# The first two pairs of a graph layer share one transposed product T from the start

## The chip, the cores and the metric

One core of a Trainium2 chip. The metric is the device time of one execution in microseconds. TensorE (PE) does the products, ScalarE (ACT), VectorE (DVE) and GpSimd (POOL) work on tiles, SyncE (SP) issues the transfers.

## The reference, cut to what matters

```python
# x (32, 256, 512) f32, adj (32, 256, 256) int32, w, wq, wk (512, 512) f32
output = einsum('bni,io->bno', x, w)
q      = einsum('bni,io->bno', x, wq)
k      = einsum('bni,io->bno', x, wk)
alpha  = einsum('bno,bmo->bnm', q, k)
alpha  = maximum(alpha, 0) * (adj != 0)
alpha  = softmax(alpha, axis=1)
y      = x + einsum('bnm,bmo->bno', alpha, output)
out    = (y - mean(y)) / sqrt(var(y) + 1e-5)
```

## The kernel before

**The algebra.** The kernel never forms q and k. It forms G from wq and wk once (with a minus sign), then for each graph T = G times x transposed, the scores S from x and T, V = x w, and O = softmax times V. The last step adds x and normalises each row. Two graphs are one *pair*; 16 pairs are numbered 0 to 15. Two pairs, 2i in *slot* 0 and 2i+1 in *slot* 1, are one *group*.

**Three products for one.** Each operand is kept as two fp32r tiles, `hi` (a rounded copy, made by ACT) and `lo` (the remainder, whole minus `hi`, made by DVE or POOL). Each product of 128x128 by 128xN is three matmuls: hi·hi, lo·hi and hi·lo (`add_chunk`, L320 to L322).

**Seven products for eight.** T (from pair 1 on) and V (from pair 1 on) are computed with seven block products P1 to P7 in place of eight. These need sums of blocks of x (S1 to S4, tile `xs`, made by POOL in four steps where S2 needs S1 and S4 needs S2), sums of blocks of G (T1, T2, T3, D4, `sum_gt` on DVE) and of w (`w_sum` on POOL). Blocks of x are A11, A12, A21, A22, those of G B11, B12, B21, B22. P1 is A11 with B11, P2 A12 with B21, P4 A22 with D4, P5 S1 with T1, P6 S2 with T2, P7 S3 with T3, P3 S4 with B22. `t_half(Pn, c, pairs)` is one 128-row half of a product: two chunks, six matmuls. A T is 14 halves, 84 matmuls. P1, P6, P5 and P3 add up in the PSUM tile `chain`; ACT copies the running sum after P1, P6 and P5 (`parts`), and DVE adds P2 (`bank_z`), P7 and P4 (`bank_y`) to the copies (`sum_t`).

**In the steady state** the loop over groups 1 to 7 runs, on PE: T of both pairs (`fill_t`, 512 columns, both slots in one matmul), O of pair 2i-1, S of pair 2i, V of pair 2i, S of pair 2i+1, O of pair 2i, V of pair 2i+1.

**The start, which the change touches**, is outside that loop. On PE: seven warm-up matmuls (L650); rows 0 to 2 of V of pair 0, plain (L497 to L503); G (`fill_g`, four quarters j of four chunks each, in `g_bank[j]`); T of pair 0, plain with 512 columns (`fill_first_t`, 16 chunks, 48 matmuls); the last row of V of pair 0; S of pair 0; T of pair 1 alone with seven products and 256 columns (`fill_second_t`); O of pair 0; S of pair 1; V of pair 1; then group 1.

Every engine runs its instructions in the order written, and semaphores order the engines. The order of the start is written out by hand for ACT (L950 to L1020), DVE (L1271 to L1341) and POOL (L1473 to L1511). After G, ACT takes G's quarters out of PSUM (`split_g`, L925), DVE makes their remainders (L1235) and the sums (`sum_gt`, L1254 and L1260), ACT casts the sums (`split_gt`, L940) and DVE makes their remainders (L1025, `g_lo<-xn,g_hi`).

Semaphores named below: `g_lo_ready` and `gt_lo_ready` count finished remainders of G's blocks and of its sums, `x_summed[slot]` POOL's sums of x, `first_s_lo_ready` and `s_lo_ready` remainders of these, `t_lo_ready` finished blocks of T, `t_copied` and `t_summed` the copies and sums of T.

## Time and profile before

| | |
|---|---|
| time, median of 3 runs | 524.33 us (523.89 to 525.05) |
| the profiled execution: its own time | 523.82 us |
| its span, first to last instruction | 522.0 us |
| mean granted TensorE clock | 0.995 |
| busy: PE, PE weight load | 98%, 89% |
| busy: DVE, ACT, POOL | 71%, 62%, 49% |

The profiled execution's time is 1.8 us more than its span and 0.5 us less than the median. Matmuls are pipelined: a matmul's duration (0.39 us with 512 columns, 0.28 us with 256) is longer than the distance from one start to the next, which is what a stream of them costs. In a timeline a row gives the start, the duration, the engine, the line and the tiles; `x4` means that four instructions are merged and the duration is theirs together; a bracket gives the idle time ahead of it and who ended it.

### The profile page before, as it was taken

The page shows a single profiled execution, that of the slowest core. Times are in us where ns is not written, and L with a number is a line of the kernel's source. Part 1 is how long each engine was busy: PE and PEld are TensorE (multiplying, and loading weights), DVE is VectorE, ACT ScalarE, POOL GpSimd, SP SyncE. Part 2 cuts the span into 40 slices and gives each one's busy share as a digit, 9 for nine tenths or more (in the row PEclk, how much of TensorE's full clock was granted, in tenths as well). Part 3 has the DMA queues.
Part 4 walks back from the last instruction along what each step waited for, and adds up shares of the span by engine and source line. Part 5 has one row for each costly group of instructions (what it writes and reads, how often), then busy time and mean ns, then how long its engine had stood idle before and what let it go on. Part 6 is the DMA issues. An engine that isn't in the chain of part 4 may idle for free.

```text
span 522.0 us, 9934 instructions
## 1 busy us (share of the span) xinstructions
PE 511.8 (98%) x3259; PEld 466.2 (89%) x3259; DVE 368.1 (71%) x746; ACT 325.8 (62%) x747; POOL 258.1 (49%) x196
## 2 busy tenths in 40 slices
PE   8999999999999999999999999999999999999994
PEld 5889998899989998899988999889998999889994
DVE  4766846776948677586866778577684867757686
ACT  5566556476763857539574586638676385764583
POOL 0397875239635386155661486433962537710011
PEclk9999999999999999999999999999999999999998
DMA  7404241044430626025350333404351061502334
GB/s 261 182 0 161 90 155 62 21 125 152 154 115 20 213 69 241 20 52 189 109 206 21 127 138 118 166 20 161 120 200 61 20 221 60 201 1 69 133 130 192
DMA packets 30735, 62.05 MB, mean 119 GB/s; under 512 B 2048, under 2 KB 3072, under 8 KB 30720
## 3 DMA queue, kind: packets, MB, share of 16 engines
q1 hardware_dynamic: 30720, 61.87, 34.2%
q8 instruction: 7, 0.11, 0.1%
q14 instruction: 8, 0.07, 0.0%
HBM read 45.09 MB, written 16.78 MB: 119 GB/s over the span
## 4 chain that ended last, share of the span: by engine, by line
PE 94%; DVE 2%; ACT 1%; DMA 1%; issue 0%; POOLq 0%; POOL 0%; SPq 0%; DVEq 0%; ACTq 0%
PE o_bank L320 12%; PE o_bank L321 12%; PE o_bank L322 12%; PE chain L320 11%; PE chain L322 11%; PE chain L321 11%; PE bank_y L320 6%; PE bank_y L321 6%; PE bank_y L322 6%; PE bank_z L320 3%; PE bank_z L321 3%; PE bank_z L322 3%; DMA xn<-in_w 1%; PE chain L502 0%; PE chain L503 0%; ACT v_hi L755 0%
## 5 line engine op out<-in xcount | busy, mean ns | idle before, releaser
L1441 POOL TENSOR_TENSOR s_lo<-xs,s_hi 128x512 fp32r<-128x512 f32 x60 | 82.6, 1394 | 33.9 <-ACT s_hi L692 33.9
L1436 POOL TENSOR_TENSOR a_lo<-xt,a_hi 128x512 fp32r<-128x512 f32 x42 | 57.9, 1386 | 61.2 <-ACT a_hi L684 61.2
L322 PE MATMUL o_bank<-t_hi,a_lo 128*128 128x256 f32 x256 | 72.4, 283 | 0.0
L321 PE MATMUL o_bank<-t_lo,a_hi 128*128 128x256 f32 x256 | 72.4, 283 | 0.0
L320 PE MATMUL o_bank<-t_hi,a_hi 128*128 128x256 f32 x256 | 72.4, 283 | 0.0
L1432 POOL TENSOR_TENSOR xs<-xt 128x512 f32<-128x512 f32 x30 | 40.0, 1347 | 47.8 <-DMA xt<-in_x_t 30.1
L1446 POOL TENSOR_TENSOR rstd<-var_eps,minus_half 128x4 f32<-128x4 f32 x14 | 14.2, 1018 | 92.6 <-DVE var_eps L1122 92.6
L711 ACT COPY parts<-chain 128x256 f32<-128x256 f32 x90 | 33.2, 370 | 39.5 <-PE chain L322 38.4
L320 PE MATMUL chain<-w_hi,s_hi 128*128 128x256 f32 x180 | 51.0, 284 | 0.5 <-ACT parts L711 0.5
L322 PE MATMUL chain<-w_hi,s_lo 128*128 128x256 f32 x180 | 50.9, 283 | 0.0
L321 PE MATMUL chain<-w_lo,s_hi 128*128 128x256 f32 x180 | 50.9, 283 | 0.0
L321 PEld LDWEIGHTS o_bank<-t_lo,a_hi 128*128 128x128 f32 x256 | 49.1, 192 | 0.3
L320 PEld LDWEIGHTS o_bank<-t_hi,a_hi 128*128 128x128 f32 x256 | 49.1, 192 | 0.3
L322 PEld LDWEIGHTS o_bank<-t_hi,a_lo 128*128 128x128 f32 x256 | 49.1, 192 | 0.0
L320 PE MATMUL o_bank<-v_hi,p_hi 128*128 128x512 f32 (+1 forms) x126 | 48.5, 385 | 0.0
L321 PE MATMUL o_bank<-v_lo,p_hi 128*128 128x512 f32 (+1 forms) x126 | 48.5, 385 | 0.0
L1037 DVE TENSOR_TENSOR parts<-parts,bank_y 128x512 f32<-128x512 f32 (+1 forms) x32 | 20.7, 653 | 39.2 <-ACT parts L701 25.8
L322 PE MATMUL o_bank<-v_hi,p_lo 128*128 128x512 f32 (+1 forms) x126 | 48.4, 384 | 0.0
L1025 DVE TENSOR_TENSOR v_lo<-parts,v_hi 128x512 fp32r<-128x512 f32 x45 | 47.6, 1071 | 0.9 <-ACT v_hi L755 0.9
L1108 DVE SCALAR_TENSOR_TENSOR xn<-o_bank,xn 128x512 f32<-128x512 f32 x60 | 40.9, 683 | 8.4 <-PE o_bank L322 8.4
L701 ACT COPY parts<-chain 128x512 f32<-128x512 f32 x42 | 24.7, 588 | 34.6 <-PE chain L322 34.1
L783 ACT ACTIVATE c_b<-xn,neg_mean 128x512 f32<-128x512 f32 x58 | 41.9, 722 | 3.4 <-DVE neg_mean L1370 2.4
(222 smaller groups left out, 1628.9 us busy)
## 6 DMA issues: line engine op xcount, KB each, us to landing
xt<-in_x_t SPq DMA_DIRECT2D x64, 256.0 KB, 3.2
...
```

Of the source, the lines that this page charges most:

```text
L320: nc.tensor.matmul(dst, a[0], b[0], start=first, stop=False, skip_group_check=shared)
L321: nc.tensor.matmul(dst, a[0], b[1], start=False, stop=False, skip_group_check=shared)
L322: return nc.tensor.matmul(dst, a[1], b[0], start=False, stop=last, skip_group_check=shared)
L701: nc.scalar.copy(parts[:, PART[product], c], chain[:, c]).then_inc(t_copied, 1)
L711: nc.scalar.copy(parts[:, PART[product], c, 0], chain_v[:, c]).then_inc(v_copied, 1)
L783: nc.scalar.activation(squares, xn[:, slot, r], ACT.Square, bias=neg_mean[:, r:r + 1], accum_out=square_sum[:, r:r + 1]).then_inc(squared, 1)
L1025: return nc.vector.tensor_tensor(dst, whole, hi.bitcast(F32), ALU.subtract)
L1037: nc.vector.tensor_tensor(part, part, bank, ALU.add).then_inc(t_summed, 1)
L1108: nc.vector.scalar_tensor_tensor(out=xn[:, slot, r], in0=row.rearrange("q j n -> q (j n)"), scalar=1.0, in1=xn[:, slot, r], op0=ALU.mult, ...
L1432: nc.gpsimd.tensor_tensor(xs[:, s], a, b, op).then_inc(x_summed[slot], 1)
L1436: nc.gpsimd.tensor_tensor(a_lo[:, slot, u], xt[:, u], a_hi[:, slot, u].bitcast(F32), ALU.subtract).then_inc(a_lo_ready[slot], 1)
L1441: nc.gpsimd.tensor_tensor(s_lo[:, slot, s], xs[:, s], s_hi[:, slot, s].bitcast(F32), ALU.subtract).then_inc(s_lo_ready[slot], 1)
```

## The change

Pairs 0 and 1 become group 0 and get one T, with seven products and 512 columns, straight behind G.

- PE: `fill_first_t` is now 14 halves of both pairs, in the order P1 P1 P2 P7 P2 P7 P6 P6 P5 P5 P3 P3 P4 P4. S of pair 0 follows (`fill_first_s`), then the last row of V of pair 0, S of pair 1 (`fill_s_b(0)`), O of pair 0 (`fill_first_o`), V of pair 1.
- SP: the four blocks of pair 1 are loaded without a wait into space that is free at the start (`x1_raw`, in `soft` and `parts`), the adjacency of pair 0 behind them, and pair 2 as soon as pair 0's sums are made.
- Sums and remainders of x for both pairs are made in the start, by POOL and DVE, between the pieces of G. wk's parts move from `a_hi[:, 1]` to `s_hi[:, 1]`.
- B12 isn't split any more (only the plain T used it).

The diff, cut to its core:

```diff
+T_FIRST = {**T_DONE, (P1, 0): 1, (P1, 1): 2, (P2, 0): 3, (P7, 0): 4, (P2, 1): 5, (P7, 1): 6}
-FIRST_A, FIRST_S = (A11, A21, A12, A22), (S3, S2, S1, S4)
+FIRST_A, FIRST_S = (A11, A12, A22, A21), (S3, S1, S2, S4)
+FIRST_LO = {S3: 1, S2: 2}, {S1: 1, S4: 2}
+G_ORDER = (T3, T2, T1, D4)
+G_SUMMED = {(T1, 0): 1, (T1, 1): 2, (T3, 0): 3, (T2, 0): 4, (T3, 1): 5, (T2, 1): 6, (D4, 0): 7, (D4, 1): 8}
...
-        wk_hi, wk_lo = a_hi[:, 1], a_lo[:, 1]
+        wk_hi, wk_lo = s_hi[:, 1], s_lo[:, 1]
+        x1_raw = {A11: soft[:, 0:M], A21: soft[:, M:R], A12: parts[:, C22, 0], A22: parts[:, C22, 1]}
-        b12 = parts[:, 0, 0]
+        b12 = c12_b
...
 SP
+            for u in (A11, A21, A12, A22):
+                sp.dma_start(x1_raw[u], x_t[1].rearrange("q (u k n) -> q u k n", u=4, k=2)[:, u]).then_inc(
+                    x1_loaded[u], 16)
+            sp.dma_start(adj[:], adj_t[0].rearrange("q (r n) -> q r n", r=R)).then_inc(adj_loaded, 16)
             sp.wait_ge(a_lo_ready[0], 4)
-            for u in range(4):
-                load_block(1, u)
-            sp.dma_start(adj[:], adj_t[0].rearrange("q (r n) -> q r n", r=R)).then_inc(adj_loaded, 16)
+            for u in (A11, A21, A22, A12):
+                sp.wait_ge(x_summed[0], READ_BY[u])
+                load_block(2, u)
             sp.wait_ge(gt_lo_ready, 4)
             load_xn(0, 0)
...
 PE
-            def fill_second_t():
+            def fill_first_t():
+                both = slice(0, 2)
+                pe.wait_ge(g_lo_ready, 2)
+                pe.wait_ge(b_lo_ready, B_LO_FIRST[A11])
+                pe.wait_ge(v_lo_ready, 2)
+                t_half(P1, 0, both)
+                t_half(P1, 1, both)
+                pe.wait_ge(g_lo_ready, 4)
+                pe.wait_ge(b_lo_ready, B_LO_FIRST[A12])
+                t_half(P2, 0, both)
+                pe.wait_ge(gt_lo_ready, G_ORDER.index(T3) + 1)
                 xs_split(S3)
+                pe.wait_ge(v_lo_ready, 3)
+                t_half(P7, 0, both)
                 pe.wait_ge(t_summed, 1)
+                t_half(P2, 1, both)
+                pe.wait_ge(gt_summed, 8)
+                t_half(P7, 1, both)
...
+            def fill_first_s():
+                pe.wait_ge(t_lo_ready, T_LO[0][A12])
+                fill_scores(0, 0)
+                pe.wait_ge(t_lo_ready, 4)
+                fill_scores(0, 1)
...
             fill_g()
             fill_first_t()
+            fill_first_s()
             fill_last_of_first_v()
-            pe.wait_ge(t_lo_ready, 4)
-            fill_scores(0, 0)
-            fill_scores(0, 1)
-            fill_second_t()
-            fill_o_b(0, first=True)
-            pe.wait_ge(t_lo_ready, 4 + T_LO[0][A12])
-            pe.wait_ge(added, 2)
-            fill_scores(1, 0)
-            pe.wait_ge(t_lo_ready, 8)
-            pe.wait_ge(added, 3)
-            fill_scores(1, 1)
+            fill_s_b(0)
+            fill_first_o()
             fill_v(1, 1, first=True)
...
 ACT, behind split_first_v(0..2)
+            split_first_a(A11)
+            split_first_s(0, S3)
+            split_first_a(A12)
+            split_g(0)
+            split_g(1)
+            split_first_s(0, S1)
+            split_first_s(0, S2)
+            split_first_a(A22)
+            split_first_a(A21)
+            split_g(2)
+            split_first_s(0, S4)
+            split_g(3)
+            split_gt(T3)
+            split_first_s(1, S3)
+            split_gt(T2)
+            split_first_s(1, S1)
+            copy_first_t(P1, 0)
+            copy_first_t(P1, 1)
+            split_first_s(1, S2)
+            split_gt(T1)
+            split_gt(D4)
+            split_first_s(1, S4)
... then the copies of P6 and P5, split_t_a, copy_c12, split_wt(T1, T3, T2), split_t_b and exponent(0, r),
... split_first_v(3), split_p(0, r), split_wt(D4), split_a(1, 0, u), split_s(1, 0, s)
 DVE, behind split_first_v(0..2)
+            split_first_b(A11)
+            split_first_s(0, S3)
+            split_first_b(A12)
+            split_g(0)
+            sum_gt(T1, 0)
+            split_g(1)
+            sum_gt(T1, 1)
+            split_first_s(0, S2)
+            split_g(2)
+            sum_gt(T3, 0)
+            sum_gt(T2, 0)
+            split_g(3)
+            sum_gt(T3, 1)
+            sum_gt(T2, 1)
+            split_first_s(1, S3)
+            split_gt(T3)
+            sum_gt(D4, 0)
+            sum_gt(D4, 1)
+            sum_t(0, A11, 0, first=True)
+            split_gt(T2)
+            split_first_s(1, S2)
+            split_gt(T1)
... then sum_t(A11, 1), split_gt(D4), sum_t(A22, 0 and 1), split_t_a(A11), split_t_a(A22),
... sum_t(A21, 0), sum_t(A21, 1), split_t_a(A12), split_t_a(A21), mask(0, 0), relu_max, split_t_b(A11), mask(0, 1),
... split_t_b(A12), relu_max, split_t_b(A22), split_t_b(A21), split_first_v(3), invert(0), split_p(0, r)
 POOL, behind the same wait on qk_lo_ready
+            sum_first_x(0, S3)
+            sum_first_x(0, S1)
+            sum_first_x(0, S2)
+            sum_first_x(1, S3)
+            split_first_s(0, S1)
+            sum_first_x(1, S1)
+            sum_first_x(0, S4)
+            sum_first_x(1, S2)
+            split_first_s(0, S4)
+            sum_first_x(1, S4)
+            split_first_s(1, S1)
+            split_first_s(1, S4)
+            split_first_a(A22)
+            split_first_a(A21)
... then w_sum as before, sum_x(1, 0, s), the remainders of w's sums (D4 last), split_a(1, 0, u), split_s(1, 0, s)
```

The new helpers are single instructions with their waits:

```python
# ACT
def split_first_s(slot, s):
    act.wait_ge(x_summed[slot], S_SUMMED[s])      # S_SUMMED = {S3: 1, S1: 2, S2: 3, S4: 4}
    if slot == 1:
        act.wait_ge(g_filled, K)
    nc.scalar.copy(s_hi[:, slot, s], xs[:, s]).then_inc(s_hi_ready[slot], 1)
# DVE
def split_first_s(slot, s):
    dve.wait_ge(s_hi_ready[slot], FIRST_S.index(s) + 1)
    rest(s_lo[:, slot, s], xs[:, s], s_hi[:, slot, s]).then_inc(first_s_lo_ready[slot], 1)
def split_first_b(u):
    dve.wait_ge(a_hi_ready[1], FIRST_A.index(u) + 1)
    rest(a_lo[:, 1, u], x1_raw[u], a_hi[:, 1, u]).then_inc(b_lo_ready, 1)
```

`sum_first_x(1, s)` on POOL also waits until the slot 0 remainder of the same s is done, because both slots use one tile `xs[:, s]`.

## Rows read from the trace of the kernel before

**Rows 1.** The page: busy time by engine, and the chain that ended last.

```profile
PE 511.8 (98%) x3259; PEld 466.2 (89%) x3259; DVE 368.1 (71%) x746; ACT 325.8 (62%) x747; POOL 258.1 (49%) x196
...
PE 94%; DVE 2%; ACT 1%; DMA 1%; issue 0%; POOLq 0%; POOL 0%; SPq 0%; DVEq 0%; ACTq 0%
```

**Rows 2.** The timeline of PE, 0 to 82 us: first matmuls of its stages.

```profile
1.45 3.36 PE L650 MATMUL o_bank<-s_hi 128*128 128x512 f32 x7 [1.45 <-DVE s_hi L1271]
...
25.55 0.39 PE L320 MATMUL chain<-a_hi,g_hi 128*128 128x512 f32 x1
...
36.43 0.39 PE L320 MATMUL o_bank<-w_hi,a_hi 128*128 128x512 f32 x1
...
39.15 0.28 PE L320 MATMUL o_bank<-t_hi,a_hi 128*128 128x256 f32 x1
...
44.90 0.28 PE L320 MATMUL bank_y<-s_hi,g_hi 128*128 128x256 f32 x1
...
60.92 0.28 PE L320 MATMUL o_bank<-t_hi,a_hi 128*128 128x256 f32 x1
...
66.67 0.28 PE L320 MATMUL chain<-w_hi,a_hi 128*128 128x256 f32 x1
...
77.54 0.40 PE L320 MATMUL bank_y<-s_hi,g_hi 128*128 128x512 f32 x1
```

**Rows 3.** The timeline of POOL, 0 to 82 us.

```profile
18.55 2.54 POOL L1432 TENSOR_TENSOR xs<-xt 128x512 f32<-128x512 f32 x2 [17.72 <-DVE a_lo L1025]
21.17 1.29 POOL L1432 TENSOR_TENSOR xs<-xs,xt 128x512 f32<-128x512 f32 x1
22.61 1.29 POOL L1432 TENSOR_TENSOR xs<-xt,xs 128x512 f32<-128x512 f32 x1
26.93 5.07 POOL L1481 TENSOR_TENSOR a_lo<-xt,a_hi 128x512 fp32r<-128x512 f32 x4 [3.03 <-ACT a_hi L970]
31.96 5.95 POOL L1441 TENSOR_TENSOR s_lo<-xs,s_hi 128x512 fp32r<-128x512 f32 x4
...
59.37 5.51 POOL L1436 TENSOR_TENSOR a_lo<-xt,a_hi 128x512 fp32r<-128x512 f32 x4
64.84 5.04 POOL L1441 TENSOR_TENSOR s_lo<-xs,s_hi 128x512 fp32r<-128x512 f32 x4
69.83 2.56 POOL L1432 TENSOR_TENSOR xs<-xt 128x512 f32<-128x512 f32 x2
74.91 1.30 POOL L1441 TENSOR_TENSOR s_lo<-xs,s_hi 128x512 fp32r<-128x512 f32 x1 [2.52 <-ACT s_hi L692]
```

**Rows 4.** The timeline of DVE, 0 to 82 us.

```profile
18.34 1.28 DVE L1025 TENSOR_TENSOR v_lo<-chain,v_hi 128x512 fp32r<-128x512 f32 x2
...
27.65 0.41 DVE L1260 SCALAR_TENSOR_TENSOR xn<-o_bank,parts 128x256 f32<-128x256 f32 x1
...
31.05 3.20 DVE L1025 TENSOR_TENSOR g_lo<-xn,g_hi 128x512 fp32r<-128x512 f32 x2 [2.00 <-ACT g_hi L940]
```

**Rows 5.** The timeline of ACT, 0 to 82 us.

```profile
17.95 0.60 ACT L923 CAST v_hi<-bank_y 128x512 fp32r<-128x512 f32 x1
...
25.75 0.60 ACT L936 ACTIVATE g_hi<-bank_z 128x512 fp32r<-128x512 f32 x1 [2.12 <-PE bank_z L322]
...
30.40 2.19 ACT L940 CAST g_hi<-xn 128x512 fp32r<-128x512 f32 x4
```

**Rows 6.** The timeline of DVE, 150 to 162 us, behind the T of a group in the loop.

```profile
158.45 0.69 DVE L1037 TENSOR_TENSOR parts<-parts,bank_y 128x512 f32<-128x512 f32 x1 [0.59 <-PE bank_y L322]
159.05 0.68 DVE L1025 TENSOR_TENSOR t_lo<-chain,t_hi 128x512 fp32r<-128x512 f32 x1
```

**Rows 7.** Windows at the end of the kernel: start:end, length, busy us of PE, PEld, DVE, ACT, POOL (instructions), granted clock, DMA share, GB/s.

```profile
514.00:516.00 2.00, 0.94 (x8) 0.73 (x7) 1.90 (x9) 1.91 (x5) 0.00 (x0) 1.00 0.00 0
516.00:518.00 2.00, 0.00 (x0) 0.00 (x0) 1.67 (x6) 0.84 (x2) 1.39 (x2) 0.81 0.00 0
518.00:522.00 4.00, 0.00 (x0) 0.00 (x0) 0.71 (x2) 0.00 (x0) 0.00 (x0) 0.50 0.68 262
```

More of the change, by code:

```diff
@@ L711, in copy_v, with split_t_a @@
                 nc.scalar.copy(parts[:, PART[product], c, 0], chain_v[:, c]).then_inc(v_copied, 1)
-            def split_t_a(i, u):
-                if u == A11:
+            def split_t_a(i, u, first=False):
+                if u == A11 and not first:
                     act.wait_ge(s_filled, 4 * i)
@@ L733, in split_t_b @@
                 if u == A12:
[L734 removed]
+                    act.wait_ge(c12_copied, i + 1)
                 whole = c12_b[:] if u == A12 else parts[:, BLOCK_AT[u], :, 1]
[L736 to L744 removed]
                 nc.scalar.copy(t_hi[:, u], whole).then_inc(t_hi_ready, 1)
@@ new lines, in _ @@
+            copy_first_t(P6, 0)
+            copy_first_t(P6, 1)
+            split_t_a(0, A11, first=True)
+            copy_first_t(P5, 0)
+            copy_first_t(P5, 1)
+            split_t_a(0, A22)
+            split_t_a(0, A12)
+            copy_c12(0, first=True)
+            split_t_a(0, A21)
+            for b in W_ORDER[:-1]:
+                split_wt(b)
+            split_t_b(0, A11)
+            split_t_b(0, A12)
+            exponent(0, 0)
+            exponent(0, 1)
+            split_t_b(0, A21)
@@ L979, in _ @@
+            exponent(0, 2)
+            exponent(0, 3)
+            split_t_b(0, A22)
             split_first_v(R - 1)
[L980 to L981 removed]
             for r in range(R):
[L983 to L994 removed]
@@ L995, in _ @@
-            split_second_t(A11)
-            split_second_t(A22)
-            split_second_t(A12)
-            split_second_t(A21)
+                split_p(0, r, first=True)
+            split_wt(D4)
             for u in (A21, A11, A12, A22):
@@ new lines, in _ @@
+            sum_gt(T2, 1)
[6 more added lines that the diff above has]
+            split_first_s(1, S2)
+            split_gt(T1)
+            sum_t(0, A11, 1, first=True)
+            split_gt(D4)
+            sum_t(0, A22, 0, first=True)
+            sum_t(0, A22, 1, first=True)
+            split_t_a(0, A11)
+            split_t_a(0, A22)
+            sum_t(0, A21, 0, first=True)
@@ new lines, in _ @@
+            sum_t(0, A21, 1, first=True)
+            split_t_a(0, A12)
+            split_t_a(0, A21)
+            dve.wait_ge(x_summed[1], 4)
+            dve.wait_ge(a_lo_ready[1], 2)
+            mask(0, 0, first=True)
+            relu_max(0, 0)
+            relu_max(0, 1)
+            split_t_b(0, A11)
+            mask(0, 1, first=True)
+            split_t_b(0, A12)
+            relu_max(0, 2)
+            relu_max(0, 3)
+            split_t_b(0, A22)
+            split_t_b(0, A21)
+            split_first_v(R - 1)
@@ L1312, in _ @@
             invert(0)
-            one = slice(1, 2)
-            sum_t(0, A11, 0, one)
             split_p(0, 0)
-            sum_t(0, A11, 1, one)
-            for r in range(1, R):
-                split_p(0, r)
-            sum_t(0, A22, 0, one)
-            sum_t(0, A22, 1, one)
-            split_second_t(A11)
-            split_second_t(A22)
-            sum_t(0, A21, 0, one)
-            sum_t(0, A21, 1, one)
-            split_second_t(A12)
-            residual(0, 0, 0, 0)
-            residual(0, 0, 0, 1)
```

299 lines of the change are left out of this document (126 added, 173 removed).

## The prediction

> **What bounds the kernel now.** I read the page's busy times and its chain first. PE is busy 98% of the span and makes up 94% of the chain that ended last, and no other engine is above 71% [rows 1]. So time is PE's instructions plus the places where PE has nothing to do, and the change touches only the stretch behind G. I then read PE's timeline as a row of stages [rows 2]: T of pair 0 starts at 25.55, V's last row at 36.43, S of pair 0 at 39.15, T of pair 1 at 44.90, S of pair 1 at 60.92, V of pair 1 at 66.67, and group 1 at 77.54. That is 51.99 us from the end of G to group 1.
>
> Two prices come out of it. With 512 columns 48 matmuls take 36.43 - 25.55 = 10.88 us, 0.227 each. With 256 columns 48 take 44.90 - 39.15 = 5.75 us, 0.120 each [rows 2]. Priced so, the work of the stretch is 10.88 (T of pair 0) + 2.72 (V's row, 12 matmuls) + 5.75 (S) + 84 x 0.120 = 10.08 (T of pair 1) + 24 x 0.227 = 5.44 (O) + 5.75 (S) + 10.08 (V) = 50.70. What is left, 51.99 - 50.70 = 1.29 us, is PE's idle time there. The stretch is nearly full, because each chain of other engines has PE work of another pair ahead of it.
>
> **What the change removes.** T of both pairs becomes 84 matmuls of 512 columns, 19.04 us, for 10.88 + 10.08 = 20.96. That is 1.92 us less. With no idle time at all, a further 1.29 would go, 3.21 in all. Everything else PE does (S, O, V, the loop) keeps its count and shape. A loss can only be new idle time of PE, and above 3.21 us of it the change costs time.
>
> **What the change adds: five places.** I follow the written order of each engine with these prices. A POOL operation on 512 elements costs 1.27 (5.07 for four), an ACT cast 0.60 to 0.62, 0.52 from start to start when they follow each other (2.19 for four), a DVE remainder with its whole in PSUM 0.64 (1.28 for two), a half-width sum on DVE 0.41 [rows 3 to 5]. A DVE remainder with both inputs in SBUF beside a busy POOL is dearer: two took 3.20, and the four POOL operations that ran then took 5.95 in place of 5.07, so POOL loses 0.44 to each [rows 3, 4].
>
> *Place 1, ahead of P2.* P1's two halves run from 25.55 to 28.27 (12 x 0.227). P2 needs all four quarters of G as remainders, and ACT's cast of the last quarter now stands behind its cast of S4 of pair 0. G's last quarter was in PSUM and its cast began at 25.75 [rows 5]. But S4 is POOL's seventh operation, POOL starts at 18.55 as before [rows 3], and 7 x 1.27 brings it to 27.4 at the earliest. DVE's four remainders from SBUF in that stretch (A11 and A12 of pair 1, S3 and S2 of pair 0) take 4 x 0.44 = 1.8 from POOL. The sum of S3 for pair 1 overwrites the tile that the second of them reads and waits some 0.3 for it. S4 is then ready at 29.5, its cast at 30.1, G's last cast at 30.75, and the DVE remainder at 31.45. PE idles from 28.27 to 31.45, **3.2 us**. Without any contention it is 27.4 + 0.6 + 0.6 + 0.65 = 29.25, 1.0 us. If DVE's remainders also push each other (1.6 each from the row, so that the one of S2 comes a POOL operation late) it is up to 4.0.
>
> The Trainium skill (SBUF — State Buffer, Who interferes with whom) says that a DVE instruction with two SBUF inputs and a GpSimd instruction that reads SBUF exclude each other for the whole instruction. Taken by that, POOL would lose a full DVE instruction each time and place 1 would be about 1 us longer; in this trace POOL lost 0.44 each and not the 0.69 of such an instruction. I keep the row.
>
> *Place 2, ahead of P7.* Behind that remainder stand T3's second half-sum (0.41), ACT's cast (0.62), ACT's cast of S3 for pair 1 (0.52 more), DVE's remainder of that and then of T3 (0.60 and 0.69 without contention), and some 0.3 of steps between engines: 3.0 to 3.2 us. P2's half covers 1.36. PE idles **1.7 us**; 1.5 with no contention, 2.9 if both DVE remainders meet POOL at 1.6 each. From here each product is ready in time: T2, T1 and D4 come 0.6 to 3 us apart and PE needs one every 2.72.
>
> *Place 3, between T and S.* S needs A12 of T, whose remainder DVE makes behind the last sum, and that sum waits for PE's last half. In the loop the same two rows follow the last half of T: the sum starts at 158.45 and the remainder ends at 159.73 [rows 6], 1.3 us plus the step from PE. There O of another pair covers it. Here nothing does: **1.4 us**, firmly (1.3 to 1.5).
>
> *Place 4, in S of pair 1.* Behind S of pair 0 PE has only V's last row, 2.72 us, for DVE and ACT to mask, take maxima, and split T of pair 1 again. By the written order DVE waits with A22 for ACT's cast, which stands behind two exponents. I get A21 done 0.3 us after PE wants it: **0.3 us** (0 to 1.5, the upper one if POOL is still at w's remainders).
>
> *Place 5, ahead of group 1.* POOL's remainder of w's D4 stands ahead of pair 2's eight remainders, and ACT casts D4 only behind the softmax of pair 0, at about 65.6. POOL starts the eight at 66.9; it started them at 59.37 before [rows 3]. They and two sums ran to 72.39, and the remainder of S3 for pair 3 ended at 76.21 after 2.52 of idle time that the delay uses up [rows 3]. Now I get 66.9 + 13.1 + 1.3 = 81.3, against PE's arrival at about 81. With contention by two DVE remainders of the next pair: **0.6 us** (0 to 1.5). The DMAs moved ahead (four blocks of pair 1 and the adjacency) stand in SP's queue behind wk as before, and only lose a wait; pair 2's blocks start at about 29 and not 44.6. I cost them at nothing: all are wanted 10 us after they land.
>
> **Sum.** -1.92 - 1.29 + 3.2 + 1.7 + 1.4 + 0.3 + 0.6 = +4.0 us. Against the profiled execution's 523.82 that is 527.8. The median of the runs stands 0.5 higher, so 524.33 + 4.0 = **528.3 us**. The ends of the terms give +0.6 to +8.1.
>
> **The rivals.**
> *The sums come in time (faster).* The one mechanism is that ACT does not wait for S4, so that place 1 is nil and place 2 at most 0.7; the point of decision is idle time below 3.21 - 1.05 = 2.16 us. Then it is 522.5. Against it: POOL's seven operations at 1.27 alone pass P1's end, and place 3 alone takes 1.4. Chance 0.05.
> *Light contention.* POOL and DVE miss each other, places 1, 2 and 3 take 1.0, 1.5 and 1.3, the others little: +0.6 to +1.7, 525.5. For it: POOL's 5.07 row has no contention. Against it: DVE has SBUF remainders back to back while POOL never stops. Chance 0.15.
> *As summed,* 528.3, chance 0.50.
> *The clock falls in place 1,* by the rows and by the page's rule above, 529.6. Against it: P1 before and P2 behind keep PE partly at work. Chance 0.22.
> *POOL's lateness goes on into group 1,* and PE waits again for S2's and S4's remainders there: 530.5 to 533. Against it: POOL is busy half the span [rows 1]. Chance 0.08.
>
> **Range and chances.** The likeliest case alone runs from 526.8 to 529.8. For eight in ten I go from 525.4, inside light contention, to 531.0. About 0.2% (1.05 us) is what a measurement of this kernel can tell from no change. Light contention lies half within it: same 0.09. Faster has 0.05, slower 0.86.
>
> **What the profile after would show.** G ends at 25.55 and P1 at 28.3. PE's first half of P2 starts at about 31.5, released by DVE's remainder of G's last quarter, behind an ACT cast that POOL's seventh `xs` released. P7 starts at 34.5, S at 50.9, V of pair 1 at 71, group 1 at 81.5, and from there the loop's period is the same. I am wrong if ACT casts G's last quarter near 26, if POOL's sums end before 27, or if group 1 starts before 78.

## The result, and the profile after

The changed kernel takes 531.49 us (median of 5 runs, 531.25 to 533.7), the kernel before 525.05 (5 runs, 523.89 to 525.4). The ratio is 1.0145, interval 1.0131 to 1.016 (it is taken over the runs and isn't the quotient of the two medians, which is 1.012). By the medians the change is 6.4 us slower, where +4.0 was predicted, and 0.5 us above the end of the range. The profiled execution is the longest of the five: 533.70 us, span 531.9. It is 9.88 above that of before.

The page of the kernel after, for [rows 1]:

```profile
PE 513.9 (97%) x3211; PEld 465.5 (88%) x3211; DVE 380.8 (72%) x750; ACT 330.0 (62%) x750; POOL 258.3 (49%) x198
...
PE 89%; DVE 2%; issue 1%; ACT 1%; POOL 1%; POOLq 0%; DVEq 0%; ACTq 0%
```

PE fell from 94% of the chain to 89%. So the loss is idle time of PE. The view of the waits, engine PE, from 25 to 90 us, names it; each row gives who waited, for whom, the sum, the number of times and the longest. Kernel after:

```profile
PE bank_y L329 <- DVE parts L1066: 3.1, 1, 3.1
PE bank_y L329 <- DVE g_lo L1047: 2.8, 1, 2.8
PE bank_z L329 <- DVE g_lo L1252: 1.5, 1, 1.5
PE o_bank L329 <- DVE t_lo L1047: 1.5, 1, 1.5
```

The same view of the kernel before, 25 to 78 us, has one row:

```profile
PE chain L320 <- ACT parts L711: 0.5, 1, 0.5
```

The first is at place 5, which the prediction priced at 0.6; the others are places 2, 1 and 3. The timeline of PE in the kernel after, for [rows 2], shows where they lie:

```profile
27.00 0.39 PE L329 MATMUL chain<-a_hi,g_hi 128*128 128x512 f32 x1
...
31.33 0.50 PE L329 MATMUL bank_z<-a_hi,g_hi 128*128 128x512 f32 x1 [1.46 <-DVE g_lo L1252]
...
35.77 0.50 PE L329 MATMUL bank_y<-s_hi,g_hi 128*128 128x512 f32 x1 [2.76 <-DVE g_lo L1047]
...
52.48 0.38 PE L329 MATMUL o_bank<-t_hi,a_hi 128*128 128x256 f32 x1 [1.45 <-DVE t_lo L1047]
...
84.28 0.39 PE L329 MATMUL bank_y<-w_hi,a_hi 128*128 128x256 f32 x1 [3.10 <-DVE parts L1066]
...
85.97 0.63 PE L329 MATMUL bank_y<-s_hi,g_hi 128*128 128x512 f32 x1
86.40 0.63 PE L330 MATMUL bank_y<-s_lo,g_hi 128*128 128x512 f32 x1
...
106.49 0.39 PE L329 MATMUL o_bank<-v_hi,p_hi 128*128 128x512 f32 x1
```

Two things beside the waits are to be seen. G ended at 27.00 and not at 25.55, because the matmuls behind the warm-up ran at half speed until 10.3 us (starts 0.43 apart in place of 0.23). And group 1 began at 85.97 with starts 0.43 apart again: T of group 1 took 106.49 - 85.97 = 20.52 where it took 19.06 before. From O of group 1 on the pieces are those of before: O starts 9.88 us later than in the kernel before (96.61), and the whole execution is 9.88 us longer.

Place 1 by engine, kernel after, for [rows 3] to [rows 5]; POOL, then ACT, then DVE:

```profile
18.65 2.55 POOL L1476 TENSOR_TENSOR xs<-xt 128x512 f32<-128x512 f32 x2 [17.81 <-DVE s_lo L1047]
...
28.12 1.28 POOL L1476 TENSOR_TENSOR xs<-xt,xs 128x512 f32<-128x512 f32 x1
```

```profile
29.44 0.62 ACT L956 CAST s_hi<-xs 128x512 fp32r<-128x512 f32 x1 [4.34 <-POOL xs L1476]
29.96 0.59 ACT L937 ACTIVATE g_hi<-bank_y 128x512 fp32r<-128x512 f32 x1
```

```profile
30.59 0.69 DVE L1252 SCALAR_TENSOR_TENSOR g_lo<-bank_y,g_hi 128x512 fp32r<-128x512 f32 x1 [2.32 <-ACT g_hi L937]
...
32.82 1.19 DVE L1047 TENSOR_TENSOR s_lo<-xs,s_hi 128x512 fp32r<-128x512 f32 x1 [0.88 <-ACT s_hi L956]
33.93 1.78 DVE L1047 TENSOR_TENSOR g_lo<-xn,g_hi 128x512 fp32r<-128x512 f32 x1
```

This is the chain of place 1 as written down: POOL's seventh sum ends at 29.40, ACT's cast of S4 and then of G's last quarter follow, DVE's remainder ends at 31.28 (31.45 in the prediction). The last two rows are place 2: both remainders met POOL, at 1.19 and 1.78 in place of 0.60 and 0.69.

And the wait of 3.1 us, DVE and then POOL of the kernel after:

```profile
79.27 4.36 DVE L1047 TENSOR_TENSOR a_lo<-xt,a_hi 128x512 fp32r<-128x512 f32 x1 [4.89 <-ACT a_hi L690]
83.55 0.68 DVE L1066 TENSOR_TENSOR parts<-parts,bank_y 128x512 f32<-128x512 f32 x1
```

```profile
67.83 5.26 POOL L1504 TENSOR_TENSOR a_lo<-xt,a_hi 128x512 fp32r<-128x512 f32 x4
73.03 5.08 POOL L1509 TENSOR_TENSOR s_lo<-xs,s_hi 128x512 fp32r<-128x512 f32 x4
78.05 2.58 POOL L1500 TENSOR_TENSOR xs<-xt 128x512 f32<-128x512 f32 x2
80.56 1.30 POOL L1509 TENSOR_TENSOR s_lo<-xs,s_hi 128x512 fp32r<-128x512 f32 x1
81.79 1.29 POOL L1500 TENSOR_TENSOR xs<-xs,xt 128x512 f32<-128x512 f32 x1
83.25 1.51 POOL L1500 TENSOR_TENSOR xs<-xt,xs 128x512 f32<-128x512 f32 x1 [0.17 <-POOL xs L1500]
```

DVE's remainder of A11 of pair 3 (both inputs in SBUF) lasted 4.36 us. POOL worked without a break under it, at its undisturbed 1.29 each, and the remainder ended 0.5 us after POOL's first pause (83.08). I call this the *hold*. The sum that P4 of V of pair 1 needs stands behind it on DVE. In the kernel before the same remainder fell into a pause of POOL (its row of 2.52 us idle ahead of 74.91 in [rows 3]); kernel before, DVE:

```profile
74.34 0.69 DVE L1025 TENSOR_TENSOR a_lo<-xt,a_hi 128x512 fp32r<-128x512 f32 x1 [5.91 <-ACT a_hi L684]
```

The windows view of the kernel after, 80 to 90 us, has a fall of the clock like the one of [rows 7]: after PE's wait for P4 the granted clock is 0.83 in the mean, between its levels of 2.4 and 1.2 GHz.

```profile
80.00:90.00 10.00, 6.90 (x34) 5.84 (x34) 9.89 (x11) 4.84 (x10) 6.39 (x5) 0.83 0.24 89
```

Behind T in the loop the rows of [rows 6] are the same in the kernel after (168.33 0.69, then 168.93 0.68).

### The profile page after: what moved, and what is told of

It reads as the page before. It is cut to its first block, busy times and chain, and to the rows that moved or that the text cites. A ratio compares the mean times of both kernels' runs of the same rounds, so it can differ in the third digit from the quotient of the medians.

```text
span 531.9 us, 9835 instructions
## 1 busy us (share of the span) xinstructions
PE 513.9 (97%) x3211; PEld 465.5 (88%) x3211; DVE 380.8 (72%) x750; ACT 330.0 (62%) x750; POOL 258.3 (49%) x198
## 4 chain that ended last, share of the span: by engine, by line
PE 89%; DVE 2%; issue 1%; ACT 1%; POOL 1%; POOLq 0%; DVEq 0%; ACTq 0%
PE o_bank L329 11%; PE o_bank L330 11%; PE o_bank L331 11%; PE chain L329 11%; PE chain L331 10%; PE chain L330 10%; PE bank_y L329 6%; PE bank_y L330 5%; PE bank_y L331 5%; PE bank_z L331 3%; PE bank_z L329 3%; PE bank_z L330 3%; POOL xs L1476 1%; DVE parts L1066 0%; DVE g_lo L1047 0%
## 5 line engine op out<-in xcount | busy, mean ns | idle before, releaser
L1509 POOL TENSOR_TENSOR s_lo<-xs,s_hi 128x512 fp32r<-128x512 f32 x56 | 75.9, 1372 | 40.0 <-ACT s_hi L698 40.0
L1059 DVE TENSOR_TENSOR parts<-parts,bank_y 128x512 f32<-128x512 f32 x32 | 22.0, 688 | 43.5 <-ACT parts L707 25.8
L1500 POOL TENSOR_TENSOR xs<-xt 128x512 f32<-128x512 f32 x28 | 36.9, 1329 | 25.2 <-DMA xt<-in_x_t 25.2
L1145 DVE TENSOR_SCALAR xn<-xn,neg_mean,rstd 128x512 f32<-128x512 f32 x56 | 41.6, 764 | 10.1 <-POOL rstd L1514 10.1
L1047 DVE TENSOR_TENSOR v_lo<-parts,v_hi 128x512 fp32r<-128x512 f32 x45 | 46.0, 1032 | 1.0 <-ACT v_hi L759 1.0
L749 ACT CAST t_hi<-parts 128x512 fp32r<-128x512 f32 x24 | 14.9, 622 | 51.2 <-PE o_bank L331 51.2
```

What stands on the lines that cost most here:

```text
L749: nc.scalar.copy(t_hi[:, u], whole).then_inc(t_hi_ready, 1)
L1047: return nc.vector.tensor_tensor(dst, whole, hi.bitcast(F32), ALU.subtract)
L1059: nc.vector.tensor_tensor(part, part, bank, ALU.add).then_inc(t_summed, 1)
L1145: nc.vector.tensor_scalar(xn[:, slot, r], xn[:, slot, r], neg_mean[:, r:r + 1], rstd[:, r:r + 1], ALU.add, ALU.mult).then_inc(normed, 1)
L1500: nc.gpsimd.tensor_tensor(xs[:, s], a, b, op).then_inc(x_summed[slot], 1)
L1509: nc.gpsimd.tensor_tensor(s_lo[:, slot, s], xs[:, s], s_hi[:, slot, s].bitcast(F32), ALU.subtract).then_inc(s_lo_ready[slot], 1)
```

## The experiments

In the table "over before" is the difference of the medians on the same chip; the ratio is again taken over the runs. Where I compare with the changed kernel, its three comparisons gave +6.4, +10.4 and +7.9 over before, so a gain against one of them alone says little below 4 us. The diffs below are against the changed kernel unless said otherwise.

| kernel | median us (range, runs) | before | over before | ratio, interval |
|---|---|---|---|---|
| after_again | 534.47 (534.08 to 534.95, 4) | 524.04 | +10.4 | 1.0188, 1.0171 to 1.0206 |
| e1_sum_first | 530.23 (530.17 to 530.29, 4) | 524.04 | +6.2 | 1.011, 1.0093 to 1.0127 |
| e2_d4_early | 529.41 (528.85 to 530.39, 4) | 524.04 | +5.4 | 1.0091, 1.0072 to 1.011 |
| e3_g_before_s4 | 531.08 (529.97 to 532.13, 4) | 524.04 | +7.0 | 1.0127, 1.0102 to 1.0152 |
| e4_fillers | 531.75 (531.13 to 532.1, 4) | 524.31 | +7.4 | 1.0131, 1.011 to 1.0152 |
| e5_port_gap | 530.99 (529.59 to 531.17, 4) | 524.31 | +6.7 | 1.0118, 1.0099 to 1.0137 |
| e6_act_order | 526.44 (526.29 to 529.56, 8) | 524.31 | +2.1 | 1.0045, 1.0026 to 1.0064 |
| e7_three | 525.15 (524.79 to 526.88, 10) | 524.31 | +0.8 | 1.0017, 1.0006 to 1.0029 |
| e8_v_between | 527.68 (524.7 to 527.92, 7) | 524.32 | +3.4 | 1.0051, 1.0032 to 1.0069 |
| e9_row_pieces | 525.59 (524.77 to 526.98, 10) | 524.32 | +1.3 | 1.0027, 1.0015 to 1.0038 |
| after_third | 532.48 (531.35 to 533.06, 4) | 524.63 | +7.9 | 1.0145, 1.0127 to 1.0163 |
| e5_again | 531.32 (528.35 to 532.37, 6) | 524.63 | +6.7 | 1.0121, 1.0099 to 1.0144 |
| e10_tail_order | 523.72 (523.33 to 525.62, 12) | 524.06 | -0.3 | 0.999, 0.9978 to 1.0003 |
| e11_v_first | 522.57 (522.28 to 522.77, 7) | 523.90 | -1.3 | 0.9973, 0.9961 to 0.9984 |

### The changed kernel once more

> The changed kernel once more, to see which of its stalls come in every execution. Theory A (a port that DVE did not get): DVE's remainder of A11 for pair 3, ahead of group 1, again takes about 4.4 us and the first matmul of P4 in V of pair 1 waits about 3 us; time 531.0 to 531.8. Rival (that one execution was unlucky): the remainder takes under 2 us, P4 waits under 1 us, and that execution's time is near 528.5.

It took 534.47, 3.0 us more than in the first comparison and more than either theory gave. Its profile (own time 534.95) has the same four waits and the hold again, at 4.25. The warm-up ended on time here and place 1 had its full length, and the clock fell twice. Waits of PE and DVE's row, then the windows, kernel after_again:

```profile
31.20 0.50 PE L329 MATMUL bank_z<-a_hi,g_hi 128*128 128x512 f32 x1 [2.68 <-DVE g_lo L1252]
35.63 0.79 PE L329 MATMUL bank_y<-s_hi,g_hi 128*128 128x512 f32 x1 [2.35 <-DVE g_lo L1047]
...
85.57 0.39 PE L329 MATMUL bank_y<-w_hi,a_hi 128*128 128x256 f32 x1 [2.99 <-DVE parts L1066]
```

```profile
80.67 4.25 DVE L1047 TENSOR_TENSOR a_lo<-xt,a_hi 128x512 fp32r<-128x512 f32 x1 [5.02 <-ACT a_hi L690]
```

```profile
30.00:40.00 10.00, 6.44 (x18) 4.70 (x19) 8.40 (x11) 5.75 (x11) 6.97 (x6) 0.66 0.08 26
...
80.00:90.00 10.00, 7.01 (x41) 6.22 (x40) 9.25 (x10) 5.94 (x12) 7.35 (x6) 0.84 0.39 143
```

P2 starts at the same absolute time in both (31.33, 31.20), though T started at 27.00 in one and 25.64 in the other. So in these two a late warm-up costs little: place 1 hides it.

### Place 5: the sum ahead of the remainder, D4's cast early, a pause on POOL

```diff
 e1, DVE                       e2, ACT
-            split_b(1, A11)   +            split_wt(D4)
             sum_v(1, A22)                  for r in range(R):
+            split_b(1, A11)                    split_p(0, r, first=True)
             sum_v(1, A11)     -            split_wt(D4)
```

> Only DVE's order ahead of group 1 differs: the sum that P4 of V waits for stands ahead of the remainder of A11 and no longer behind it. Theory A: the wait of P4 (3.1 us) goes, PE's clock no longer falls behind it (1.5 us), and the time drops by 3 to 4.6 us, to 527 to 528.5. Rival (group 1 waits for POOL's remainders anyway, as the prediction had it in place 5): PE waits at group 1's first halves instead, and the drop is under 2 us.

> ACT casts w's D4 ahead of the four softmax casts of pair 0 and not behind them, so that POOL starts pair 2's remainders earlier by 1.7 to 3.2 us. Theory B (POOL's lateness is what hurts ahead of group 1): its stream is over before DVE comes with the remainder of A11, the remainder is short, and the drop is 3 to 4.6 us. Rival (it only moves the softmax casts back by one cast): O of pair 0 starts 0.5 us later and nothing is gained at P4, 0 to +0.5 us.

Both take P4's wait away, as both theories said, and against after_again on the same chip they save 4.2 and 5.1 us (3 to 4.6 expected of each). Against the +6.4 and +7.9 of the other two comparisons of the changed kernel they save 0.2 and 1.7 (e1), 1.0 and 2.5 (e2). In e1 the remainder takes 1.68, but behind the sum. In e2 POOL starts earlier, has a pause when the remainder comes, and it takes 0.69 again. Kernel e2_d4_early, DVE, then POOL:

```profile
80.92 0.69 DVE L1047 TENSOR_TENSOR a_lo<-xt,a_hi 128x512 fp32r<-128x512 f32 x1 [5.00 <-ACT a_hi L690]
```

```profile
78.35 2.56 POOL L1500 TENSOR_TENSOR xs<-xt 128x512 f32<-128x512 f32 x2
81.48 1.30 POOL L1509 TENSOR_TENSOR s_lo<-xs,s_hi 128x512 fp32r<-128x512 f32 x1 [0.57 <-ACT s_hi L698]
```

Group 1 starts at 84.01 and 84.11 with no wait ahead of P4, 3.2 us earlier than in after_again, and its T runs at the full clock from the start (starts 0.23 apart), which is 1.4 more.

```diff
 e5, POOL
             sum_x(1, 1, S1)
+            pool.wait_ge(b_lo_ready, 3)
             split_s(1, 1, S3)
```

> POOL waits, ahead of its remainder of S3 for pair 3, until DVE's remainder of A11 for the same pair is done. Theory A (DVE is kept from the port by POOL's unbroken row of operations): the remainder takes at most 1.8 us in place of 4.3, P4's wait in V of pair 1 falls from 3 us to under 0.8, and the time drops by 2 to 4 us. Rival (the 4.3 us have another cause, such as data that is late): the remainder still takes over 3 us and the time rises by what POOL now loses.

With POOL held back for that one remainder it takes 1.89 (from 79.23), PE's wait shrinks from 3.10 to 0.63, and group 1 starts at 83.31. But e3 and e4 below, whose DVE and POOL have the order of the changed kernel, have no hold either (1.78 and 1.89), and e5's median is within 0.8 us of e4's. The rows fit theory A: in both holds and in e5 the remainder ended 0.55 us after POOL's first pause began (at 83.08, 84.37 and 80.58). But an execution of the edit without a hold shows nothing by itself where the unedited order also runs without one, and the time didn't show the expected gain of 2 to 4 us either: +6.7 lies above the +6.4 of the first comparison. So that POOL's row keeps DVE out is argued from the rows; how often it does is the next question.

### Is the hold in every execution?

The changed kernel and e5 on one chip, and two more single executions of the changed kernel, each with its profile:

> The changed kernel, unedited, beside e5's edit on one chip. In two profiles DVE's remainder of A11 of pair 3 was held from 79.27 and 80.67 for 4.36 and 4.25 us; in e3 and e4, whose DVE and POOL orders are the same, it took 1.78 and 1.89. Theory A (the hold is a property of this order and timing, and is in nearly every execution of the changed kernel): the profile shows it again at over 4 us, group 1 starts 3.4 us after V's end of work, and the median lies 2.5 to 4.5 us above that of e5_again. Rival B (it is a chance event that profiled executions happened to show): the profile may show 1.8 us, and the median lies within 1.5 us of e5_again.

> POOL waits for the remainder before its own third operation, as in e5_port_gap. The hold can't occur. By both theories the remainder takes under 2 us and the time is 5 to 7 us above the kernel before; theory A puts it 2.5 to 4.5 us below after_third, rival B within 1.5 us.

> The changed kernel, one more profile on the same chip. Theory A: the remainder takes over 4 us. Rival B: under 2 us here or in after_third or after_fifth. Where it takes under 2 us the time should be about 2.6 us less by the wait and 1.4 by the clock.

> The changed kernel, one more profile on the same chip, for the same question. Theory A: over 4 us. Rival B: a mixture over the three.

Theory A fell. The median of after_third is 1.2 us above that of e5_again, the intervals of their ratios overlap, and the remainder took 1.78, 1.80 and 1.89 in the three profiles (own times 532.90, 531.50, 530.77). The hold is in two of five profiles of the changed kernel. The orders are the same; in after_fifth DVE gets through at the first border between two POOL operations, behind the two sums, and POOL's next operation grows to 1.73. Without a hold PE's wait is short, and it is again for DVE's sum behind that remainder. Kernel after_fifth, PE, then DVE, then POOL:

```profile
82.57 0.39 PE L329 MATMUL bank_y<-w_hi,a_hi 128*128 128x256 f32 x1 [0.62 <-DVE parts L1066]
```

```profile
80.03 1.89 DVE L1047 TENSOR_TENSOR a_lo<-xt,a_hi 128x512 fp32r<-128x512 f32 x1 [4.90 <-ACT a_hi L690]
```

```profile
78.82 2.55 POOL L1500 TENSOR_TENSOR xs<-xt 128x512 f32<-128x512 f32 x2
81.32 1.73 POOL L1509 TENSOR_TENSOR s_lo<-xs,s_hi 128x512 fp32r<-128x512 f32 x1
83.01 1.30 POOL L1500 TENSOR_TENSOR xs<-xs,xt 128x512 f32<-128x512 f32 x1
```

The clock varies as much: it stayed at 1.00 in after_fifth in every window, through waits of 1.92 and 2.77 us, and was lowest in after_third. Windows, kernel after_third:

```profile
30.00:40.00 10.00, 6.71 (x15) 4.85 (x16) 8.21 (x11) 6.21 (x12) 6.95 (x6) 0.59 0.07 26
40.00:50.00 10.00, 10.00 (x41) 8.15 (x41) 2.90 (x5) 2.87 (x5) 9.84 (x8) 0.90 0.28 105
```

### Place 1: who waits on ACT

```diff
 e3, ACT
             split_g(2)
-            split_first_s(0, S4)
             split_g(3)
+            split_first_s(0, S4)
             split_gt(T3)
```

> ACT casts G's last quarter ahead of S4 of pair 0. Theory C (place 1 of the prediction: PE waits at P2 because ACT waits for POOL's seventh sum): PE's wait ahead of P2 (1.6 us in the profile after, 1.5 more hidden by a late warm-up) goes, P7 starts 1.5 to 2.2 us earlier, because the cast of T3 still stands behind S4, and the time drops by 1.5 to 2.2 us. Rival (T3's own chain sets P7): P7 starts less than 0.5 us earlier and the time stays within 0.5 us.

Kernel e3_g_before_s4, PE:

```profile
28.99 0.43 PE L329 MATMUL bank_z<-a_hi,g_hi 128*128 128x512 f32 x1
...
34.34 0.79 PE L329 MATMUL bank_y<-s_hi,g_hi 128*128 128x512 f32 x1 [3.78 <-DVE g_lo L1047]
```

Place 1 is gone (P2 starts at 28.99 with no wait), so its cause was S4 on ACT. But P7 comes only 1.3 us earlier than in after_again (34.34 for 35.63), a little less than theory C had: T3's cast still stands behind S4's, and PE's wait went there, 3.78 us long. The clock fell in it (0.66 from 30 to 40 us), and S of pair 0 starts only 0.3 earlier (53.61 for 53.94), though T had started 0.6 later here (26.27 for 25.64). The time is 3.4 below after_again, more than the 1.5 to 2.2 expected, but nearly all of that is place 5, where there was no hold here (1.78), P4 waits 0.52, and T of group 1 runs at the full clock.

```diff
 e6, ACT
-            split_first_s(0, S4)
             split_g(3)
-            split_gt(T3)
             split_first_s(1, S3)
+            split_gt(T3)
             split_gt(T2)
+            split_first_s(0, S4)
             split_first_s(1, S1)
```

> ACT's order between G and T alone: G's last quarter, S3 of pair 1, T3 and T2 are all cast ahead of S4 of pair 0. Theory C (that one cast, behind POOL's seventh sum, makes places 1 and 2): P7's first matmul starts at 31 to 32.5 and not at 35.7, PE's clock doesn't fall there, and the time drops by 4 to 6 us against the changed kernel. Rival (DVE's port collisions or POOL's sums set T3 anyway): P7 starts later than 34 and the drop is under 2 us.

S4 goes behind T3 and T2 as well. Waits of PE, kernel e6_act_order:

```profile
28.79 0.50 PE L329 MATMUL bank_z<-a_hi,g_hi 128*128 128x512 f32 x1 [0.32 <-DVE g_lo L1252]
31.74 0.50 PE L329 MATMUL bank_y<-s_hi,g_hi 128*128 128x512 f32 x1 [1.29 <-DVE g_lo L1047]
48.44 0.39 PE L329 MATMUL o_bank<-t_hi,a_hi 128*128 128x256 f32 x1 [1.45 <-DVE t_lo L1047]
78.03 0.38 PE L329 MATMUL bank_y<-w_hi,a_hi 128*128 128x256 f32 x1 [0.62 <-DVE parts L1066]
```

P7 starts at 31.74, as theory C said. The two places shrink from 5.9 us together (in after_again, by the starts, as in the table further down) to 2.1, the clock stays at 1.00 in every window of the profile, and the time is 2.1 us above before, 4.3 us less than the smallest excess of the changed kernel.

> The order of e6_act_order, the sum of e1_sum_first ahead of the remainder, and w's D4 cast as in e2_d4_early. If the places add up, the gains do too: 4 to 6 us, 3 us and up to 1 us off, which gives 523 to 526, about the kernel before. Rival (what is won at the front is given back, because POOL is then as late as before ahead of group 1): the gain is no more than e6_act_order's.

e7 is e6 with e1 and e2. P4's wait goes, and +0.8 us is left, inside the expected 523 to 526 us. Its waits are 0.37 (P2), 1.30 (P7) and 1.45 (S), 3.1 together, as much as the change can save.

### Is it the clock, or the idle time?

```diff
 e4, PE: idle products of 512 columns, which nothing reads
             t_half(P1, 1, both)
+            pe.wait_ge(gt_summed, 2)
+            fillers(10)
             pe.wait_ge(g_lo_ready, 4)
...
             t_half(P2, 0, both)
+            fillers(10)
...
+                    pe.wait_ge(added, R)
+                    fillers(11, w_hi[:, 0])       # ahead of P4 of V of pair 1
```

> The changed kernel with extra matmuls whose results nobody reads, at the places where PE waits: 10 of 512 columns ahead of P2, 10 ahead of P7, 11 ahead of P4 in V of pair 1 (about 2.3 us each, less than each wait). Theory D (PE's clock falls because of these waits, and that costs 1.5 to 3 us): the granted clock stays at its upper level from the warm-up to the end, and the time is 1.5 to 4 us below the changed kernel's of the same day (531.5 to 534.5), though no wait is any shorter. Rival (the clock falls for another reason, or costs nothing since the waits hide it): same time within 0.5 us, or more by the fillers.

The granted clock is 1.00 in each window from 10 to 90 us (the page's mean 0.997), and the kernel is still 7.4 us slower than before. So the waits cost most of what the change loses without any fall of the clock; 2.5 us of the 7.4 are the idle products ahead of P4, where the wait without a hold is 0.8. The saving of 1.5 to 4 us that I expected isn't shown: the changed kernel did not run on this chip, and +7.4 lies between its +6.4 and +10.4. What a fall of the clock costs is read from rows instead, in the table of the section on the prediction.

### Cover for the three places

```diff
 e9, PE, against e7: the row's four chunks as cover
             t_half(P1, 1, both)
+            pe.wait_ge(gt_summed, 1)
+            last_row_chunk(0)
...
             t_half(P2, 0, both)
+            last_row_chunk(1)
+            last_row_chunk(2)
...
             t_half(P7, 0, both)
...
             fill_first_t()
+            last_row_chunk(3)
             fill_first_s()
-            fill_last_of_first_v()
             fill_s_b(0)
 e8, PE, against e9: V of pair 1 between the two S
             fill_first_s()
+            fill_v(1, 1, first=True)
             fill_s_b(0)
             fill_first_o()
-            fill_v(1, 1, first=True)
```

In e8 the written orders of ACT, DVE and POOL follow PE's new order, with D4 cast ahead of T's second half.

> e7_three with only the chunks of V's last row moved into the three waits, and nothing in their old place between S of pair 0 and S of pair 1. Theory E: the waits at P2, P7 and ahead of S shrink by some 2.7 us together, and the same 2.7 us come back as a wait in S of pair 1, whose T still has to be split: time within 1 us of e7_three. Rival (the row was no cover, S of pair 1 is ready anyway): 2 to 2.7 us less than e7_three, 522.5 to 523.

> Built on e6_act_order and e1_sum_first, with PE's work laid where it waits: the four chunks of V's last row go one ahead of P2, two ahead of P7 and one ahead of S of pair 0, and V of pair 1 goes between S of pair 0 and S of pair 1, as the loop has it; ACT, DVE and POOL follow that order. Theory E (what the change lacked was PE work as cover, the 1.9 us of work that it saves are real): PE's idle time behind G falls to under 1.5 us, group 1 starts at 75 to 76.5 and the time is 1 to 2.5 us below the kernel before, 521.8 to 523.3. Rival (POOL can't have pair 2's and 3's remainders ready that early): group 1 waits for them and starts at 77.5 or later, no gain.

In e9 places 1 and 2 are covered, place 3 shrinks to 0.77, and a wait of 1.76 comes up ahead of S of pair 1, which the row had covered; the clock fell behind it (0.83 from 50 to 60 us). Kernel e9_row_pieces, PE:

```profile
48.30 0.39 PE L329 MATMUL o_bank<-t_hi,a_hi 128*128 128x256 f32 x1 [0.77 <-DVE t_lo L1050]
56.08 0.39 PE L329 MATMUL o_bank<-t_hi,a_hi 128*128 128x256 f32 x1 [1.76 <-DVE t_lo L1050]
```

It stands 1.3 above before and e7 0.8, so the two are within 1 us of each other, as theory E had it. In e8 V of pair 1 covers that chain too, but the tail's order, made for the old place of V, leaves a wait of 2.12 at group 1's P1, and the clock falls there (0.83 from 80 to 90). Group 1 started at 76.89, and the expected time below the kernel before was missed by far: +3.4. The seven executions of e8 are one of 524.70 with a mean granted clock of 0.997 and six of 527.12 to 527.92 with 0.993 or 0.994.

```diff
 e10, ACT, against e8
-            for r in range(R):
-                exponent(1, r)
+            act.wait_ge(s_filled, 4)
             split_a(1, 1, A11)
-            split_s(1, 1, S3)
             split_a(1, 1, A12)
+            exponent(1, 0)
+            split_s(1, 1, S3)
+            for r in range(1, R):
+                exponent(1, r)
 e10, DVE
             residual(0, 0, 0, 0)
             split_b(1, A11)
-            for r in range(1, R):
-                residual(0, 0, 0, r)
+            residual(0, 0, 0, 1)
             split_b(1, A12)
-            means(0, first=True)
+            residual(0, 0, 0, 2)
             invert(1)
+            residual(0, 0, 0, 3)
             split_v(1, A12, V_AT[1])
+            means(0, first=True)
 e11, DVE, against e10
             split_b(1, A12)
+            split_v(1, A12, V_AT[1])
+            invert(1)
             residual(0, 0, 0, 2)
-            invert(1)
             residual(0, 0, 0, 3)
-            split_v(1, A12, V_AT[1])
             means(0, first=True)
```

> e8_v_between with two orders mended ahead of group 1: ACT casts A11, A12 and S3 of pair 3 ahead of three of the four exponents of pair 1, and DVE makes the last residual row and the remainder of V's A12 ahead of the means. In e8_v_between PE waited 0.6 us ahead of group 1, 2.3 us ahead of its P1 and its clock fell there. Theory E: both waits go, the clock holds, and the time is 521.5 to 523, under the kernel before. Rival (the start only hands its lateness on to the next place, whatever the order): another wait of 1 us or more appears in group 1 and the time stays at 524 or above.

Group 1 starts at 75.57, 1.97 us earlier than in the kernel before. One wait of 1.41 at its P1 gives most of it back, and the time equals that of before within the interval: not the 521.5 to 523 of theory E, and the new wait is the one that the rival had. The remainder that it waits for starts on DVE at 77.60, behind two rows of the residual. Kernel e10_tail_order, PE:

```profile
78.51 0.49 PE L329 MATMUL chain<-a_hi,g_hi 128*128 128x512 f32 x1 [1.41 <-DVE v_lo L1052]
```

> DVE's remainder of A12 of V of pair 1 moves ahead of the third and fourth rows of the residual of pair 0; nothing else differs from e10. In e10 PE stood 1.57 us at group 1's first product (76.93 to 78.51), which wants the bank that this remainder reads; ACT's cast for it had ended at 76.36, and DVE made the remainder only at 77.60, behind two rows and the inversion. Theory A (what is left after place 1 to 5 is the order of DVE's work, not its amount): the remainder starts at about 76.4 and the first product at about 77.1 to 77.3, so the wait shrinks from 1.57 to about 0.3 us, the profiled span falls by 1.2 to 1.3 us and the time to about 522.5, 1.5 below the kernel before (ratio 0.997). Rival B (the 1.2 us only moves: the third and fourth rows of the residual free banks or columns later and PE waits in group 1 for them): the time stays at e10's, within 0.3 us of the kernel before.

Theory A held in the main. The remainder starts at 76.72, the wait is 0.22, the span is 0.8 us shorter than e10's (1.2 to 1.3 expected), and the median is 522.57, 1.3 us below the kernel before; the whole interval lies below 1. Kernel e11_v_first, PE:

```profile
48.74 0.39 PE L329 MATMUL o_bank<-t_hi,a_hi 128*128 128x256 f32 x1 [0.77 <-DVE t_lo L1052]
77.64 0.49 PE L329 MATMUL chain<-a_hi,g_hi 128*128 128x512 f32 x1 [0.22 <-DVE v_lo L1052]
```

From T to group 1 e11 has about as much idle time as the kernel before (1.4 and 1.3 us) and takes 1.8 us less. So the change's 1.92 us of saved work are real, and what ate them was cover and order.

## Why the prediction was wrong

The direction was right, and so was the mechanism at places 1 to 3: cover is lost, and PE waits there for the instructions named. Three steps failed: place 2 was sized at 1.7 us and cost 3.1; the clock was held at its upper level in the sum and fell in four of five profiles; and place 5 had another cause than the one given, which cost 3.4 to 3.5 us where the hold came. The time lay 3.2 us above the forecast, 0.7 of it because the kernel before also took 525.05 beside it and not 524.33. The table takes PE's lost time from the starts in the five profiles of the changed kernel, with the work priced as in the prediction. Place 1 is P2's start less T's start less 2.72, place 2 is P7's start less P2's less 1.36, place 3 is S less P7 less 14.98 (66 x 0.227), place 4 is V of pair 1 less S less 19.66, place 5 is group 1 less V less 10.08, and the row on group 1 is O less T less 19.06.

| us | predicted | after | again | third | fourth | fifth |
|---|---|---|---|---|---|---|
| G's end later than 25.55 | 0 | 1.4 | 0.1 | 0.5 | 1.0 | 1.8 |
| place 1 | 3.2 | 1.6 | 2.8 | 2.9 | 2.2 | 2.1 |
| place 2 | 1.7 | 3.1 | 3.1 | 3.1 | 3.1 | 3.1 |
| place 3 | 1.4 | 1.7 | 3.3 | 4.5 | 3.3 | 1.7 |
| place 4 | 0.3 | 0.3 | 0.2 | 0.2 | 0.2 | 0.2 |
| place 5 | 0.6 | 3.5 | 3.4 | 0.8 | 0.8 | 0.9 |
| T of group 1 | 0 | 1.5 | 1.4 | 0.4 | 0.4 | 0.4 |
| saved | -3.2 | -3.2 | -3.2 | -3.2 | -3.2 | -3.2 |
| sum | 4.0 | 9.9 | 11.1 | 9.1 | 7.7 | 6.9 |
| own time less 523.82 | | 9.9 | 11.1 | 9.1 | 7.7 | 6.9 |

Each entry is rounded by itself. The sums meet the times of the executions, so nothing is lost outside the table.

- *What the change removes, -1.92 and -1.29.* Right. In e11, where PE has cover, the stretch from 25.72 to group 1 at 75.90 is 50.18 us, 1.81 shorter than the 51.99 of before, with 1.4 us of idle time in it.
- *Place 1, 3.2.* Right in chain, in start (31.45 against 31.20 to 32.13) and in size. POOL's seventh sum came at 29.40 in after against 29.5, partly by luck: contention took some 1.0 us from POOL and not 1.8 (its sums at 21.27, 23.62 and 26.59 took 1.6 each), and POOL stood still for 0.85 and not 0.3. A late warm-up shifts its time into the first row and leaves the sum of the two at 2.9 to 3.9. e3 shows the cause.
- *Place 2, 1.7, is the step that failed in size, in every profile by 1.4.* I took remainders of 0.60 and 0.69 with a little contention; both met POOL (1.19 and 1.78). The upper bound of 2.9 that I gave for just that was added up wrong too: with 3.20 for the pair, in a row of [rows 4], my own terms give 0.41 + 0.62 + 0.52 + 3.20 + 0.3 - 1.36 = 3.7 us. Those were the nearest rows, and the measured 3.1 lies between.
- *Place 3, 1.4.* It cost 1.7 where the clock holds, 0.3 above, and up to 4.5 where T's matmuls behind places 1 and 2 run at 1.2 GHz. *Place 4* was right.
- *Place 5, 0.6.* 0.8 to 0.9 in three profiles, and that the size fits there is luck. I had PE wait for POOL's remainder of S3 of pair 3. POOL was as late as I had it (it was to end at 81.3 and ended at 81.86 in after), but PE never waited for it in the changed kernel: in after_fifth it ended at 83.05 and group 1 began at 84.10, with no wait there. What PE waited for is DVE's sum ahead of P4, inside V of pair 1, because the remainder in front of it took 1.8 to 1.9 us beside POOL. In two profiles the hold adds 2.6. I had not priced it: I asked whether POOL's products come in time, and not what its moved row lies over. With the sum first (e1) or D4 early (e2) the row is 0.0.
- *T of group 1, 0.* In the three profiles without a hold it took 0.4 more, at the full clock. The first matmul of its P1 comes 0.49 us behind the one before it in after_fifth (85.75), just after DVE's remainder that reads the same bank has ended (85.52); e10 and e11 show the same wait at 1.41 and 0.22. The row is 0.0 in e1, e2 and e5.
- *The clock, a rival with 0.22, was the likelier case.* It fell in four of five profiles: behind place 1 in after_again and after_third, behind place 2 in after_fourth, at place 5 in after and after_again, for 1.5 (after), 3.0 (again), 2.8 (third) and 1.6 us (fourth) in all: place 3 above 1.7, and T of group 1 where it ran at 1.2 GHz. The prediction's price for a fall, 1.3, was a little below the smallest. The Trainium skill (TensorE: Matmul & The Clock Gate, Part 1: The HAM clock gate) has the clock fall after an idle stretch; the four profiles agree, and after_fifth has such stretches at the full clock.

With place 2 at 3.1 and one fall of the clock at 1.5 the sum of the prediction is 4.0 + 1.4 + 1.5 = 6.9, against 6.4 and 7.9 in the first and the last comparison; this is put together afterwards and foretells nothing. Why after_again's four runs lie 2 to 3 us higher isn't shown; its one profile has the hold and two falls of the clock.
